# Causal masks of the score tiles moved from TensorE to VectorE, with a new order of the work of a head

## What is computed

```
q, k, v = heads(xn @ Wq) / 8, heads(xn @ Wk), heads(xn @ Wv)
sim  = where(causal, -max, q @ k.T)
attn = softmax(sim)
out  = attn @ v
adj  = clip(attn + eye, 0, 1);  deg = sum(adj)
feats = v
for l in (0, 1):
    h = feats @ gnn_w[l] + gnn_b[l]
    feats = gelu((adj @ h) / deg + feats)
out = out + feats @ lin_w + lin_b
```

## Time and profile before

| | us |
|---|---|
| median of 3 runs (lowest, highest) | 1555.07 (1554.51, 1558.55) |
| the profiled execution | 1548.79 |
| its span | 1547.0 |
| TensorE busy | 1411.9 (91%) |
| VectorE busy | 1247.2 (81%) |
| ScalarE busy | 1008.0 (65%) |
| GpSimd busy | 361.8 (23%) |

### The profile page before, as it was taken

The page is one execution under the profiler, slowest core; times in us unless marked ns, Lnnn a source line. Parts: engine busy times, 40 slices in busy tenths (PEclk is TensorE's granted clock), DMA queues, the critical chain, the costliest instruction groups (busy, mean ns, idle before and its releaser), DMA issues. The chain is left out here.

```text
span 1547.0 us, 28982 instructions
## 1 busy us (share of the span) xinstructions
PE 1411.9 (91%) x9944; PEld 1097.0 (71%) x9944; DVE 1247.2 (81%) x3495; ACT 1008.0 (65%) x2376; POOL 361.8 (23%) x474
## 2 busy tenths in 40 slices
PE   5999999999999999999999999999878999999896
PEld 4677777877777877777777787777455666666663
DVE  6688887878878888888888888885788888888875
ACT  2566666666666666666666666666366776778573
POOL 2012222111221112222222212222222332222211
PEclk8999999999999999999999999998898999999999
DMA  5111212111121111211111211220300000000100
GB/s 132 25 31 29 58 34 50 28 29 28 35 49 29 28 29 32 45 36 28 28 32 34 47 28 29 59 49 1 92 22 17 23 19 21 22 18 22 28 12 21
DMA packets 40668, 53.30 MB, mean 34 GB/s; under 512 B 11678, under 2 KB 23882, under 8 KB 40522
## 3 DMA queue, kind: packets, MB, share of 16 engines
q1 hardware_dynamic: 40522, 51.46, 15.0%
HBM read 9.89 MB, written 1.05 MB: 7 GB/s over the span
## 5 line engine op out<-in xcount | busy, mean ns | idle before, releaser
L1146 ACT ACTIVATE t<-PS 128x512 f32<-128x512 f32 (+3 forms) x384 | 189.1, 492 | 140.3 <-PE PS L685 90.8
L1654 DVE TENSOR_TENSOR t<-t 128x512 fp32r<-128x512 f32 (+3 forms) x384 | 209.9, 553 | 8.5 <-ACT t L1147 5.1
L1637 DVE TENSOR_REDUCE t<-PS 128x1 f32<-128x512 f32 (+3 forms) x384 | 203.6, 550 | 13.2 <-PE PS L656 9.0
L1147 ACT ACTIVATE t<-PS 128x512 fp32r<-128x512 f32 (+3 forms) x384 | 188.5, 491 | 0.0
L735 PE MATMUL PS<-t 128*128 128x512 f32 (+3 forms) x384 | 150.3, 391 | 41.2 <-ACT t L1180 21.6
L656 PE MATMUL PS<-t 128*128 128x512 f32 (+3 forms) x384 | 144.6, 379 | 15.6 <-DMA t<-t 9.9
L1303 ACT ACTIVATE t<-PS,t 128x128 f32<-128x128 f32 x256 | 113.3, 464 | 68.0 <-DVE t L1915 68.0
L1443 POOL TENSOR_TENSOR t<-t 128x256 f32<-128x256 f32 x64 | 39.4, 615 | 496.1 <-DVE t L1674 496.1
L682 PE MATMUL PS<-t 128*128 128x512 f32 (+3 forms) x384 | 145.1, 378 | 2.2 <-DMA t<-t 2.2
L1477 POOL TENSOR_TENSOR t<-t 128x16 f32<-128x16 f32 x32 | 92.8, 2901 | 231.9 <-DVE t L1759 231.9
L683 PE MATMUL PS<-t 65*128 65x512 f32 (+3 forms) x384 | 134.6, 351 | 0.0
(11 more groups left out here) (204 smaller groups left out, 3854.4 us busy)
## 6 DMA issues: line engine op xcount, KB each, us to landing
t<-t SPq DMA_DIRECT2D x184, 128.0 KB, 2.3
t<-t SPq DMA_DIRECT2D x62, 256.0 KB, 3.3
t<-in_c_rot SPq DMA_DIRECT2D x4, 512.0 KB, 5.1
t<-in_L_ffn_wqkv SPq DMA_DIRECT2D x2, 768.0 KB, 6.8
t<-in_L_attn_Wv SPq DMA_DIRECT2D x2, 512.0 KB, 7.7
out<-t SPq DMA_DIRECT2D x4, 256.0 KB, 2.3
t<-in_L_ffn_w SPq DMA_DIRECT2D x2, 341.0 KB
t<-in_L_attn_x SPq DMA_DIRECT2D x2, 256.0 KB, 3.0
```

The costliest lines, as they stand in the source:

```text
L1146: e.activation(Es[:, k % NS, 0:n], b[:, 0:n], ACT.Exp).then_inc(a_es.up((t, k)), 1)
L1147: e.activation(Eh[:, o:o + n], b[:, 0:n], ACT.Exp).then_inc(a_eh.up((t, k)), 1)
L1637: e.tensor_reduce(n[:, c, ib:ib + 1], bank(k % 2)[:, 0:hi - lo], AX.X, ALU.max, negate=True).then_inc(d_max.up((t, k)), 1)
L1654: e.tensor_tensor(El[:, o:o + n], Es[:, k % NS, 0:n], f32(Eh[:, o:o + n]), ALU.subtract).then_inc(d_el.up((t, k)), 1)
```

## The change

On diagonal tiles TensorE's third product goes, and with it the table cmB and VectorE's copy that made it. A new function on VectorE, `acausal(t, k)`, adds the mask to the tile's first 128 columns in PSUM and raises a new semaphore d_sm; ScalarE waits for it instead of for TensorE. The other waits of ScalarE's `scores` are now written ahead of this one. GpSimd's bias addition waits for one more thing, the next head's first half of VectorE's `feats`. The call lists of TensorE, ScalarE and VectorE within a round are reordered.

```diff
 # tensor
                 b = bank(2 + k % 2)
-                diag = jb >= 4 * c
                 e.matmul(b[:, 0:n], K1[r][:, jb * P:(jb + 1) * P], Q1[r][:, i0:i0 + n], start=True, stop=False)
-                m = e.matmul(b[:, 0:n], K2[r][:, jb * P:(jb + 1) * P], Q2[r][:, i0:i0 + n], start=False, stop=not diag)
-                if diag:
-                    m = e.matmul(b[:, 0:P], identB[:], cmB[:, 1, :], start=False, stop=True)
-                m.then_inc(p_sc.up((t, k)), 1)
+                e.matmul(b[:, 0:n], K2[r][:, jb * P:(jb + 1) * P], Q2[r][:, i0:i0 + n], start=False,
+                         stop=True).then_inc(p_sc.up((t, k)), 1)
...
 # scalar
-                q.wait_ge(*p_sc[t, k])
                 q.wait_ge(*(d_el[t, k - NS] if k >= NS else d_el[t - 1, k + NTL - NS]))
                 q.wait_ge(*p_hop[t - 1, k])
+                q.wait_ge(*(d_sm if jb >= 4 * c else p_sc)[t, k])
                 e.activation(Es[:, k % NS, 0:n], b[:, 0:n], ACT.Exp).then_inc(a_es.up((t, k)), 1)
...
-                exp_table(t)
                 scores(t, 0)
...
                 scores(t, 4)
...
+                exp_table(t)
+                scores(t, 5)
...
 # gpsimd
                 q.wait_ge(*d_f2[t, 1])
+                if t + 1 < NH:
+                    q.wait_ge(*d_f2[t + 1, 0])
                 e.tensor_tensor(fF[u][:], fF[u][:], gb[:, 1:2, :].broadcast_to([P, 8, DH]), ALU.add).then_inc(w_fb.up(t), 1)
...
 # vector
+            def acausal(t, k):
+                if t >= NH:
+                    return
+                q.wait_ge(ld["cm"], 16)
+                q.wait_ge(*p_sc[t, k])
+                s = bank(2 + k % 2)[:, 0:P]
+                e.tensor_tensor(s, s, cm[:, 1, :], ALU.add).then_inc(d_sm.up((t, k)), 1)
...
+                acausal(t, 0)
+                acausal(t, 1)
                 scores(t, 0)
...
+                acausal(t, 8)
                 projv(t + 1, 0)
                 causal(t + 1, 6)
-                scores(t, 7)
+                acausal(t, 9)
```

More of the change, by code:

```diff
@@ L298, in program @@
         d_cm = signal("d_cm", maskings)
+        d_sm = signal("d_sm", [(t, k) for t, k in by_tile if tiles[k][1] >= 4 * tiles[k][0]])
         d_nm = signal("d_nm", heads)
@@ L848, in tensor @@
                 scores(t, 5)
-                tail(t - 2, 1)
+                av(t, 1)
+                av(t, 2)
+                scores(t, 6)
+                graph2(t - 1, 10)
                 smax(t + 1, 4)
@@ L868, in tensor @@
                     linear(5, 7)
-                smax(t + 1, 8)
-                scores(t, 9)
-                scores(t, 10)
-                smax(t + 1, 9)
+                scores(t, 11)
+                av(t, 6)
                 graph1(t, 0)
-                scores(t, 11)
                 proj(t + 2, 0, 2)
-                av(t, 6)
                 av(t, 9)
                 av(t, 7)
-                proj(t + 2, 1, 3)
+                av(t, 8)
                 graph2b(t - 1)
@@ L882, in tensor @@
                     qkv(0)
-                av(t, 8)
+                av(t, 10)
                 smax(t + 1, 11)
-                av(t, 10)
                 av(t, 11)
+                proj(t + 2, 1, 3)
+                smax(t + 1, 10)
+                graph1(t, 1)
                 graph2(t, 0)
-                smax(t + 1, 10)
                 graph2(t, 2)
-                graph1(t, 1)
                 graph2(t, 1)
@@ L1234, in scalar @@
                 scores(t, 2)
+                tailT(t - 2, 0)
                 scores(t, 3)
@@ L1833, in vector @@
                     began(1)
+                acausal(t, 2)
                 smax(t + 1, 0)
                 scores(t, 1)
-                scores(t, 2)
-                scores(t, 3)
                 causal(t + 1, 1)
-                causal(t + 1, 2)
+                acausal(t, 3)
                 smax(t + 1, 1)
@@ L1842, in vector @@
                     linear(0, 7)
+                scores(t, 2)
+                causal(t + 1, 2)
+                scores(t, 3)
                 smax(t + 1, 2)
+                scores(t, 4)
+                causal(t + 1, 3)
                 tail(t - 2, 0)
-                share(t - 1, 1)
-                causal(t + 1, 3)
                 smax(t + 1, 3)
-                scores(t, 4)
+                scores(t, 5)
                 smax(t + 1, 4)
                 tail(t - 2, 1)
+                share(t - 1, 1)
                 smax(t + 1, 5)
@@ L1869, in vector @@
                 scores(t, 10)
-                causal(t + 1, 9)
-                smax(t + 1, 8)
                 graph1(t, 0)
@@ L1875, in vector @@
                 feats(t, 0)
+                lower(t + 2, 0, 2)
+                causal(t + 1, 11)
                 graph2b(t - 1)
-                lower(t + 2, 0, 2)
+                share(t, 0)
+                smax(t + 1, 11)
+                causal(t + 1, 10)
                 lower(t + 2, 1, 3)
-                causal(t + 1, 11)
-                causal(t + 1, 10)
-                smax(t + 1, 11)
                 smax(t + 1, 10)
-                share(t, 0)
                 graph1(t, 1)
```

74 lines of the change are left out of this document (37 added, 37 removed).

## The result

| | before | after |
|---|---|---|
| median of 4 runs (lowest, highest) | 1555.85 (1554.51, 1558.55) | 1580.16 (1570.39, 1587.95) |
| the profiled execution | 1548.79 | 1575.68 |
| its span | 1547.0 | 1573.9 |
| mean granted clock, share of 2.4 GHz | 0.978 | 0.964 |

What follows compares the result with a forecast made beforehand. TensorE was read as the fullest engine (91%), VectorE next (81%). Plain terms of -14 us and extra rounds of +17 gave +3, say +4: 1553 us profiled, median 1559; own range 1547 to 1575, whole range 1533 to 1587.

Steps and rivals of the forecast that it cites:

- load and smaller hole against masks: The forecast's mechanism, chance 0.50: table load and VectorE's smaller hole eat what the masks give, between -8 and +20 us.
- rival 1: VectorE's row becomes the bound in every head, each handover costing 0.1 us more than reckoned: 1585 us, slower; chance 0.17.
- the plain rounds: Rounds without VectorE's extra work: -0.4 us a head, -14 us over 32 heads, with periods of 31.5 us.
- the table load: Start of each head: ScalarE's load stands behind the d_sm wait, so TensorE loses 1.3 us waiting for tile 0.
- Rival 3: Head start: the chip starts the load ahead of the separate wait, hiding it: 42 us less, 1518 us; chance 0.08.
- Rival 4: Head start: a load that is waited for costs a second 1.3 us each head: 42 us more, 1600 us; chance 0.03.
- the wait before `graph2(t, 0)`: End of a head: TensorE's wait for VectorE goes, since `graph2b` comes 1.0 us earlier: -0.7 us a head.
- the masks: Diagonal score tiles: dropping the mask product saves TensorE 0.13 us each, eight a head: -1.04 us.
- rival 2: The masks' gain arrives: VectorE's hole is larger than reckoned, extra rounds cost no more than before: 1537 us; chance 0.22.
- the extra rounds: Rounds with extra VectorE work: its hole is 1.0 us instead of 2.00, TensorE waits at `smax(t + 1, 8)`; periods 33.2 us.
- 1.0 more in each of 16 rounds: +16 us, +19 at most: Extra rounds: 1.76 us of extra work sticks out instead of 0.76, and TensorE waits for it; +19 with later masks.

## Why the prediction was right and wrong

The sign was forecast, and the median, 1580, lies in the whole range of 1533 to 1587. The mechanism named, load and smaller hole against masks, is what the trace shows. The size of the loss was not: +4 forecast, +24 measured, which is outside the forecast's own range (at most +20, 1547 to 1575) and nearer to the 1585 of rival 1, whose mechanism (VectorE bounds every head) the plain rounds don't show. More than half of the loss, 15.4 us, came by the clock, which no term of the sum has; that the median still lies in the whole range is luck.

*Right: the table load.* Forecast 1.0 after `scores(t, 0)`, TensorE idle 1.2 to 1.3: the trace has 1.07 and, in most heads, 1.24, and the two runs that move the load gain 1.27 a head, 41 us in all, where 1.3 was the term. Rival 3 (load hidden) stood at 1518 and would have needed the load ahead of a wait that is an instruction of its own; none of the 31 loads was. Rival 4 is out too: the exponential starts 1.29 after the load (530.08, 531.37), as it does in the runs with an early load, so a load that is waited for costs nothing beyond its 1.28. The rule of ScalarE: Activation LUTs in the Trainium skill (What ACT_TABLE_LOAD costs), with a drain of 1.38 behind it, was not borne out; the measurement decides.

*Right in kind, too small: the wait before `graph2(t, 0)`.* -0.7 was the term; GpSimd's wait alone gives -0.93 to -1.03 a head on the kernel before. It frees VectorE of 1.0. Where TensorE gets more of it than the 0.7 counted was not traced further.

*Too large: the masks.* -1.04 a head was the distance of starts in the earlier trace rows, eight times. Measured 0.12 a head with the late load and 0.3 to 0.5 without. The step that was mis-sized is "a mask costs TensorE 0.13, eight of them 1.04": the starts were read right, but the handover to VectorE takes part back. Tile 0 alone loses 0.52 by it (TensorE's stall 1.24 against 0.72), and that handover I had put into the term of the load. Without it the masks are worth 0.12 + 0.52 = 0.64 with the late load.

*Partly luck: the plain rounds.* 31.5 was forecast and 31.65 measured, but from 31.89, a round of before in which TensorE waits for no transfer. In like rounds the gain is 0.22 a head and not 0.44: the masks gave some 0.5 less than reckoned and the wait before `graph2(t, 0)` 0.3 more, and these errors cancel in good part. The average of rounds 6 to 17 fell by 0.65, more than half of it because the waits for transfers went (4.4 us in the twelve). The prediction has these in rival 2 and not in its sum.

*Right at full clock: the extra rounds.* Forecast: 33.2, no hole left before the mask of tile 8, TensorE idle at `smax(t + 1, 8)`. Measured: 33.1 to 33.6, no idle before line 1648 at 706.66, 1.29 + 0.15 idle. VectorE's hole in plain rounds was 0.80, forecast 1.0. Over 16 rounds the extra cost came to +10.8 where I had +17 with -7 for the plain part of the same rounds, so +10. The 0.78 that an extra round of before was longer came from one pair of rounds; the averages of rounds 18 to 29 and 6 to 17 differ by 0.47 before, and after by 1.8 with the cost of the half clock taken out.

*What failed.* The step of the prediction that failed is the term "1.0 more in each of 16 rounds: +16 us, +19 at most": it priced a stall of TensorE at its own length. In seven of the 16 rounds a stretch at 1.2 GHz followed, and those seven cost another 15.4 us, more than what the sixteen extra rounds lost at full clock (10.8). The rows read of before gave no such case: the window of a head has a granted clock of 1.00, and TensorE's holes are 0.54 and 0.68. The trace of before has one, in round 30. And I gave the upper bound of the term from the stall alone, although the mean granted clock of before, 0.978, says that the level does drop in this kernel somewhere.

What is shown of the cause: each of the 15 stretches in rounds 2 to 29 of the changed kernel's two executions starts within 1.4 us of the end of the stall, and they are much more frequent behind the stall of 1.3 than behind that of 0.8 to 1.0; the stretches moved to the head's start when the stall did; they went when it went, in two kernels, while TensorE was busier than ever there. So the fall follows stalls that stand right ahead of it, whatever the place. What is not shown: how much idle time is enough and why rounds with like stalls differ. The stall of 1.24 at the start of the plain rounds has no fall behind it, 0.54 and 0.68 close together have one in half of the plain rounds of another kernel, and stalls of 1.7 to 1.9 in half of the cases. The run that was to fill the stall at equal order did not fill it.

*Left out: start and end.* Head 1 begins 5.1 later. 1.1 of it is only where the load is seen in a head; the other 4.0 go with a stretch of half clock at the start that lasts 27 us instead of 17. That stretch lasted from 14 to 44 us over the profiled runs, and 44 and 27 for the same kernel, so it cannot be put down to the change; it also spreads the times of all kernels. From head 31 to the first exponential of the second part 63.8 us pass instead of 58.4, though the load from which this is counted stands 1.1 later. In round 31 TensorE has idle times of 1.24, 0.27, 0.59 and 0.82 in the first 13 us, and the last 32 us before the second part are granted 0.74 of full clock, where the last 27 of before have 0.88. The runs differ here too (the kernel with the early load has 59.0), and how much belongs to the change stays open. The second part itself takes the same time in both.

## What to carry to other kernels

A stall of the engine that bounds a kernel may cost more than its own length: on TensorE look at the granted clock behind the longest stalls, and remove or move such a stall before saving cycles elsewhere. An average over rounds can hide waits that come and go; compare like rounds. On an engine with function tables, look in the compiled order where each load stands relative to the waits; which wait is written first decided some 40 us here. When several edits come in one change, run each alone: here the two lines on GpSimd were worth 2% by themselves, and the load in the wrong place hid that.

## What the runs showed of the hardware

The granted clock of TensorE fell to half within 1.4 us of the end of stalls of 0.8 to 1.4 us in the changed kernel, of an engine that was 90% busy around them, for 3.4 or 6.8 us at a time (once 10.2 in the kernel with the early load). In the version without GpSimd's wait it fell behind two stalls of 0.54 and 0.68, 1.9 us apart. It cost about 0.45 us for each microsecond at half clock (13.9 for 30.7), and nothing in the old order with VectorE's masks (rounds of 34.1 with and without). At the start of the kernel the half-clock stretch lasted between 14 and 44 us in executions of kernels whose starts are alike, which moves the whole time by up to some 12 us.

A copy of 256 columns on VectorE, with both inputs in SBUF, took 1.48 beside GpSimd's addition of 512 columns and mostly 0.41 to 0.50 without it, in both orders. GPSIMD Engine Reference in the Trainium skill (Specifications) has this contention for VectorE instructions with two SBUF inputs. The traces agree; here it is three times the copy's duration, for an addition that had no hurry.
